# Experts' loop of a ViT tower with a mixture of experts: the one-hot table behind the second silu, and the down products in another order

## The chip, the cores and the metric

One core of a Trainium2 chip (trn2) runs the whole program in one launch. The metric is the device time of the execution in microseconds (us), the median of several runs.

## What is computed

The program is an image tower: a tokenizer with windowed attention, a second attention with a top-k mask, and then a mixture-of-experts layer over 2,080 tokens (32 images of 65) of 192 features. The change touches the last part alone. Cut to that part, the reference is:

```python
xb = x[token_buf].reshape(E, CAP, H)              # rows of each expert: E = 128, CAP = 192, H = 192
gu = jnp.einsum('ech,ehf->ecf', xb, W_gate_up)    # f = 2 * 464
g, u = jnp.split(gu, 2, axis=-1)
inter = jax.nn.silu(g) * u
yb = jnp.einsum('eci,eih->ech', inter, W_down)    # i = 464
yb = yb * w_buf.reshape(E, CAP, 1)
routed = jnp.zeros((T, H), x.dtype).at[token_buf].add(yb.reshape(E * CAP, H))
shared = jax.nn.silu(x @ Wsg) * (x @ Wsu) @ Wsd
return (routed + shared).reshape(B, S, H)
```

Only experts to which a token was routed are worked on. With these inputs there are 20 of them, in 10 passes of a loop of two.

## The kernel before

The first three quarters of the program (tokenizer, attentions, router, shared expert) go tile by tile, in an order of stages that is written out by hand. The experts' loop follows. Each engine has its own copy of the loop (`Fori`, 10 passes, `s` = 0 and 1 inside), its instructions stand in program order, and the engines wait for each other by semaphores alone. `v` numbers the experts from 1, and most buffers come in two, by `s`.

For expert `v` the engines do this:

- **TensorE (PE).** Gate and up products in two halves `r` = 0 and 1. Each half has 4 products over the first 128 features (L999) and 4 over the other 64 (L1004), into the banks `big[r]`; the semaphore `eup{r}` tells that a half is done. Between the halves, and behind the L1004 of the first, stands `slots_of` (L928): 34 small bf16 products of a one-hot table that is two experts ahead give the rows' numbers and weights. Behind the second half come four transposes of the next expert's gathered rows (`gathered`, L937, semaphore `xe_T`), and then the down products, again by halves of the inner features. A half waits for `einner{r}`, and has two products with 128 columns of rows (L1014), and two with the other 64 rows (L1017). These last two go to partitions 0 to 63 and 64 to 127 of one bank and are called a pair here. A matmul of float32 shows as two records in the trace.
- **ScalarE (ACT).** The tanh of each half (L1195), the copy of the transposed rows to SBUF (L1125, `xeT_ready`, for the next expert), and, once `down_mm` is there, the scaled result `y` (L1199, L1200, semaphore `y_early`).
- **VectorE (DVE).** For each half the silu (L1636) and the product with `u` (L1640), which sends `einner{r}`. Behind the first half: two small copies for the add (L1644, L1645), `indices_of` (L1559 to L1565), which makes the row numbers for GpSimd's gather, and the generator `slots_of`, which makes the one-hot table of expert `v + 3`. `slots_of` reads the expert's number (L1540, `value_load`), copies its slots (L1542, `twice`), compares them with a row of numbers for tiles 0 to 7 (L1548, 128x1536) and yields. The rest of it, tiles 8 to 16 (L1548, 128x1728) and a copy of weights (L1552, `hot_ready`), runs behind the second half. Last comes the upper part of `y` (L1652), which waits for `y_early` and sends `y_done`.
- **GpSimd (POOL).** The gathers of expert `v + 2` (L1769), behind `index_ready`, and the adds of `y` to the output by indirect DMA (L1807), behind `y_done`.
- **SyncE (SP).** The loads of an expert's weights, one expert ahead: gate and up behind `eup1`, down behind `down_mm`.

The PSUM banks are `lists_bank` (p_small, one per `s`) for the row lists and transposes, and `aux` (p_small for one `s`, p_shared for the other) for the down products. They are four banks.

Of the kernel before, what the change touches and what calls it, by code (L numbers as in the profile page):

```python
# [6 lines left out]
D = 192  # L7
# [6 lines left out]
E, TOPE, CAP = 128, 6, 192  # L14
# [15 lines left out]
NSC, NIC = IS // SC, I // SC  # L30
# [302 lines left out]
def tower_kernel(nc, a, out):  # L333
# [4 lines left out]
    with ctx:  # L338
# [18 lines left out]
        def carve(start, rows, *dims, dt=f32):  # L357

            n = 1
            for d in dims:  # L360
                n *= d
            n = n if dt == f32 else n // 2
            views = [x[0:rows, start:start + n] for x in arena]
            if dt != f32:
                views = [x.bitcast(dt) for x in views]
            if len(dims) == 2:
                views = [x.rearrange("p (a b) -> p a b", b=dims[1]) for x in views]
            return views, start + n
# [146 lines left out]
        w_dn, at = carve(at, SC, NIC, D)  # L515
        xg, at = carve(at, 128, 2, DX)
        einner, at = carve(at, SC, NIC, CAP)
# [8 lines left out]
        lists_bank, aux = [small[1], small[2]], [small[0], sh_bank]  # L526
# [15 lines left out]
        def S(name):  # L542
            return named[name]
# [128 lines left out]
        def _(pe):  # L672
            mm, tr = nc.tensor.matmul, nc.tensor.transpose
# [250 lines left out]
            def slots_of(s, v):  # L924
                pe.wait_ge(S("hot_ready"), v)
                for h in range(2):
                    for t in range(NT):
                        last = mm(lists_bank[s][:, 400 + 6 * h:406 + 6 * h], hot[s][:, t, 128 * h:128 * h + 128], rhs[s][:, t, :],  # L928
                                  start=(t == 0), stop=(t == NT - 1))
                last.then_inc(S("index_mm"), 1)  # L930

            def gathered(s, gather_value, v):
                pe.wait_ge(S(f"gathered{s}"), gather_value)
                for h in range(2):
                    for k in range(2):
                        rows = PARTS[h].stop - PARTS[h].start
                        last = tr(lists_bank[s][:, k * CAP + 128 * h:k * CAP + 128 * h + rows],  # L937
                                  xg[s][0:rows, h, k * 128:(k + 1) * 128], ident[0:rows, 0:rows])
                last.then_inc(S("xe_T"), 1)
# [49 lines left out]
            with pe.Fori(0, n2) as i:  # L989
                for s in range(2):  # L990
                    v = 2 * i + s + 1
                    pe.wait_ge(S(f"w_loaded{s}"), 80 * i + 80)
                    pe.wait_ge(S("xeT_ready"), v)
                    for r in range(2):
                        pe.wait_ge(S(f"einner{r}"), v)
                        for j in range(2):
                            for bank in range(2):
                                c = bank * I + (2 * r + j) * SC
                                mm(big[r][0:SC, bank, j * CAP:(j + 1) * CAP], w_gu[s][:, c:c + SC], xeT[s][:, 0, :],  # L999
                                   start=(j == 0), stop=False)  # L1000
                        for j in range(2):
                            c = (2 * r + j) * SC
                            for bank, rows in enumerate((slice(0, DB), slice(DB, 2 * DB))):
                                last = mm(big[r][0:SC, bank, j * CAP:(j + 1) * CAP], w_gu_late[s][rows, c:c + SC],  # L1004
                                          xeT[s][rows, 1, :], start=False, stop=(j == 1))
                        last.then_inc(S(f"eup{r}"), 1)
                        if r == 0:
                            slots_of(s, v + 2)
                    gathered(1 - s, 32 * i + 32 + 32 * s, v + 1)
                    pe.wait_ge(S("y_done"), v)  # L1010
                    for r in range(2):
                        pe.wait_ge(S(f"einner{r}"), v + 1)
                        for c in range(2 * r, 2 * r + 2):
                            mm(aux[s][:, 0:D], einner[s][:, c, 0:128], w_dn[s][:, c, :], start=(c == 0), stop=False)  # L1014
                        for c in range(2 * r, 2 * r + 2):
                            half = slice(64 * (c % 2), 64 * (c % 2) + 64)
                            last = mm(aux[s][half, D:2 * D], einner[s][:, c, 128:CAP], w_dn[s][:, c, :],  # L1017
                                      start=False, stop=(c >= NIC - 2))
                    last.then_inc(S("down_mm"), 1)

# [182 lines left out]
        def _(dve):  # L1204
# [330 lines left out]
                tt(h3_cls[:], small[1][0:B, 0:D], cls_row[:], ALU.add).then_inc(S("c_h3_ready"), 1)  # L1535
                yield from router_in(1, 1, B)

            def slots_of(j, s, v):

                e = dve.value_load(lists[0:1, bass.ds(j, 1)] if not isinstance(j, int) else lists[0:1, j:j + 1],  # L1540
                                   min_val=0, max_val=E)
                V.tensor_copy(slot_twice[s][:], slot[:, :, bass.ds(e, 1)].to_broadcast([128, NT, 2])).then_inc(S("twice"), 1)  # L1542
                dve.wait_ge(S("twice"), v)
                pairs = "p t (c two) -> p t c two"
                for tiles in (slice(0, HOT_FIRST), slice(HOT_FIRST, NT)):
                    n = tiles.stop - tiles.start
                    shape = [128, n, CAP // 2, 2]
                    tt(hot[s][:, tiles, 0:CAP].rearrange(pairs, two=2),  # L1548
                       iota_b[:].rearrange("p (c two) -> p c two", two=2).unsqueeze(1).to_broadcast(shape),
                       slot_twice[s][:, tiles, :].unsqueeze(2).to_broadcast(shape), ALU.is_equal)  # L1550
                    if tiles.stop == NT:
                        V.tensor_copy(rhs[s][:, :, 3:6], wsplit[:, :, bass.ds(e, 1), :].squeeze(2)).then_inc(S("hot_ready"), 1)  # L1552
                    yield

            def indices_of(s, v):

                dve.wait_ge(S("index_mm"), v)
                p = lists_bank[s][:, 400:412].rearrange("p (h c) -> p h c", c=6)
                stt(slot_a[s][:].unsqueeze(2), p[:, :, 2:3], 1.0, dummy_f[:].unsqueeze(2), ALU.subtract, ALU.mult)  # L1559
                V.reduce_sum(slot_w[s][:].unsqueeze(2), p[:, :, 3:6], axis=AX.X)  # L1560
                V.tensor_copy(slot_b[s][:].unsqueeze(2), p[:, :, 1:2]).then_inc(S("index_part"), 1)
                dve.wait_ge(S("index_part"), 2 * v - 1)
                tt(slot_a[s][:], slot_a[s][:], slot_b[s][:], ALU.add).then_inc(S("index_part"), 1)
                dve.wait_ge(S("index_part"), 2 * v)
                stt(index[s][:].unsqueeze(2), p[:, :, 0:1], 64.0, slot_a[s][:].unsqueeze(2), ALU.mult, ALU.add)\  # L1565
                    .then_inc(S("index_ready"), 1)
# [62 lines left out]
            with dve.Fori(0, n2) as i:  # L1629
                for s in range(2):  # L1630
                    v = 2 * i + s + 1
                    slots = slots_of(2 * i + s + 3, 1 - s, v + 3)
                    for r in range(2):
                        g, u = (big[r][0:SC, b, 0:2 * CAP] for b in range(2))
                        dve.wait_ge(S(f"eth{r}"), v)
                        stt(eth[r][:], eth[r][:], 1.0, g, ALU.add, ALU.mult).then_inc(S("esilu"), 1)  # L1636
                        dve.wait_ge(S("esilu"), 2 * v - 1 + r)
                        if r == 0:
                            dve.wait_ge(S("down_mm"), v)
                        tt(einner[s][:, 2 * r:2 * r + 2, :].rearrange("p c n -> p (c n)"), eth[r][:], u, ALU.mult)\  # L1640
                            .then_inc(S(f"einner{r}"), 1)
                        if r == 0:
                            dve.wait_ge(S("add_done"), v)
                            V.tensor_copy(add_index[s][:], index[s][:])  # L1644
                            ts(add_w[s][:], slot_w[s][:], 0.5, None, op0=ALU.mult).then_inc(S("kept"), 1)  # L1645
                            dve.wait_ge(S("kept"), v)
                            indices_of(s, v + 2)
                        if r == 0:
                            next(slots)
                    run(slots)  # L1650
                    dve.wait_ge(S("y_early"), v)
                    stt(y[s][0:64, 1, :], aux[s][64:128, D:2 * D], add_w[s][0:64, 1:2], y[s][0:64, 1, :], ALU.mult, ALU.add)\  # L1652
                        .then_inc(S("y_done"), 1)
# [235 lines left out]
```

## Time and profile before

| | |
|---|---|
| median of 3 runs | 936.86 us (936.58 to 936.96) |
| the profiled execution | 934.52 us |
| its span, first to last instruction | 932.7 us |
| experts' loop, from the first L999 to the end of the last L1017 | about 186 us of it, 20 experts |
| PE, DVE, ACT, POOL busy over the span | 89%, 77%, 37%, 33% |

The profiled execution stands 2.34 us under the median, of which the span leaves out 1.8 us ahead of the first and behind the last instruction. Busy time is an average over stages with different limits. The loop is read by itself in what follows: rows of one expert in order of time, which tell at each step what started when, and what it had waited for.

### The profile page before, as it was taken

How to read it: one execution, taken by the hardware profiler on the slowest of the kernel's cores; microseconds unless marked ns; L12 is line 12 of the kernel's file. 1: busy time of each engine (PE TensorE's matmuls, PEld its weight loads, DVE VectorE, ACT ScalarE, POOL GpSimd, SP SyncE). 2: the span in 40 equal slices, each digit the busy share in tenths (PEclk: the TensorE clock that was granted, in tenths of full speed). 3: DMA queues.
4: the chain of work that ended last, by engine and by line, in shares of the span. 5: the costliest groups of instructions: out<-in, count | busy, mean ns of one | idle time of the engine just before them, and what ended most of it. 6: DMA issues, size and time to landing. Idle time of an engine off the chain costs nothing.

```text
span 932.7 us, 22271 instructions
## 1 busy us (share of the span) xinstructions
PE 830.9 (89%) x7603; PEld 731.8 (78%) x7603; DVE 722.6 (77%) x3781; ACT 345.7 (37%) x971; POOL 307.7 (33%) x354
## 2 busy tenths in 40 slices
PE   1687899899899899899899999999999999999993
PEld 1576688788788788888789989998879767676762
DVE  3356899999899899999999979799675465656562
ACT  0335554544544544545445344432210122222220
POOL 7021213403313223224123131121121276766664
PEclk8699999999999999999999999999998899999997
DMA  7410000101101101001001100010112466666651
GB/s 222 117 52 1 2 27 23 40 17 37 30 17 36 30 11 39 17 24 34 26 23 44 31 6 21 22 45 20 45 28 64 112 160 144 160 144 160 144 129 24
DMA packets 48231, 54.25 MB, mean 58 GB/s; under 512 B 9013, under 2 KB 41531, under 8 KB 48108
## 3 DMA queue, kind: packets, MB, share of 16 engines
q1 hardware_dynamic: 39180, 43.89, 16.4%
q0 software_dynamic: 6352, 7.62, 5.6%
q10 hardware_dynamic: 2608, 1.60, 0.7%
q8 instruction: 48, 0.79, 0.4%
q14 instruction: 43, 0.35, 0.1%
HBM read 42.40 MB, written 10.69 MB: 57 GB/s over the span
## 4 chain that ended last, share of the span: by engine, by line
DVE 48%; PE 38%; issue 5%; ACT 4%; SPq 2%; DVEq 1%; POOL 0%; DMA 0%; ACTq 0%; POOLq 0%
DVE b_arena L1500 9%; PE p_big L999 3%; PE p_shared L831 3%; DVE b_top_a L1486 3%; PE p_big L686 3%; PE p_shared L832 3%; PE p_big L687 2%; DVE b_top_d L1486 2%; PE p_shared L837 2%; DVE b_arena L1548 2%; DVE b_top_b L1486 2%; DVE b_top_c L1486 2%; PE p_small L693 2%; DVE b_rstd L1238 2%; PE p_big L1004 2%
## 5 line engine op out<-in xcount | busy, mean ns | idle before, releaser
L1769 POOL DMA_INDIRECT b_arena<-x_rows,b_index x44 | 68.0, 1544 | 49.4 <-DVE b_index L1565 36.6
L686 PE MATMUL p_big<-b_xT,b_ff1a 128*128 128x128 f32 x384 | 77.5, 285 | 1.4 <-ACT b_xT L1029 1.4
L1703 POOL TENSOR_TENSOR b_arena<-b_kY,b_mask_k 64x256 f32<-64x256 f32 x16 | 9.7, 608 | 205.9 <-ACT b_kY L1054 205.9
L687 PE MATMUL p_big<-b_xT,b_ff1b 128*128 128x128 f32 x384 | 76.5, 282 | 0.0
L1029 ACT COPY b_xT<-p_small 128x256 f32<-128x256 f32 (+1 forms) x97 | 35.4, 377 | 83.4 <-PE p_small L677 83.3
L1734 POOL TENSOR_TENSOR b_arena<-b_arena 128x768 f32<-128x768 f32 x16 | 27.0, 1687 | 117.8 <-DVE b_arena L1512 117.8
L686 PEld LDWEIGHTS p_big<-b_xT,b_ff1a 128*128 128x128 f32 x384 | 61.6, 200 | 2.5 <-ACT b_xT L1029 2.5
L999 PE MATMUL p_big<-b_xeT,b_arena 128*116 128x192 f32 x320 | 61.9, 336 | 0.0
L687 PEld LDWEIGHTS p_big<-b_xT,b_ff1b 128*128 128x128 f32 x384 | 60.7, 199 | 0.0
L720 PE MATMUL p_big<-b_arena,b_q_blk 128*128 128x256 f32 (+3 forms) x256 | 48.9, 334 | 12.5 <-ACT b_q_blk L1061 12.4
L720 PEld LDWEIGHTS p_big<-b_arena,b_q_blk 128*128 128x128 f32 x256 | 41.3, 190 | 19.4 <-POOL b_arena L1703 12.6
L999 PEld LDWEIGHTS p_big<-b_xeT,b_arena 128*116 128x116 f32 x320 | 50.1, 180 | 5.6 <-issue 5.6
L867 PE MATMUL p_small<-b_patch_w,b_xp 128*128 128x192 f32 x192 | 36.8, 344 | 12.1 <-DMA b_pe<-in_pe 10.3
L1548 DVE TENSOR_TENSOR b_arena<-b_iota_b,b_slot_twice 128x1536 bf16<-128x1536 bf16 (+1 forms) x46 | 46.1, 1005 | 0.8
L1111 ACT ACTIVATE b_th<-p_shared 116x256 f32<-116x256 f32 (+1 forms) x50 | 18.9, 378 | 69.6 <-PE p_shared L832 62.1
L867 PEld LDWEIGHTS p_small<-b_patch_w,b_xp 128*128 128x128 f32 x192 | 32.5, 198 | 13.4 <-issue 10.2
L1500 DVE MATCH_REPLACE8 b_arena<-b_top_c,b_arena 128x65 f32<-128x65 f32 x208 | 41.7, 210 | 0.0
L1500 DVE MATCH_REPLACE8 b_arena<-b_top_b,b_arena 128x65 f32<-128x65 f32 x208 | 41.2, 211 | 0.0
L1500 DVE MATCH_REPLACE8 b_arena<-b_top_a,b_arena 128x65 f32<-128x65 f32 x208 | 41.2, 212 | 0.0
L837 PE MATMUL p_shared<-b_wsd,b_inner 116*128 116x192 f32 (+1 forms) x208 | 39.9, 349 | 0.8 <-DVE b_inner L1316 0.8
L1078 ACT ACTIVATE b_arena<-b_arena 128x768 f32<-128x768 f32 (+1 forms) x32 | 28.1, 877 | 31.6 <-DVE b_arena L1448 17.8
L1807 POOL DMA_INDIRECT out_rows<-b_hid,b_add_index x20 | 30.6, 1532 | 25.2 <-issue 25.2
(379 smaller groups left out, 2548.1 us busy)
## 6 DMA issues: line engine op xcount, KB each, us to landing
b_arena<-in_w_gate_up SPq DMA_DIRECT2D x20, 464.0 KB
b_arena<-in_w_down SPq DMA_DIRECT2D x20, 336.0 KB
b_xp<-in_xp SPq DMA_DIRECT2D x16, 384.0 KB, 3.1
b_arena<-in_w_gate_up SPq DMA_DIRECT2D x40, 116.0 KB
xT_rows<-b_xmT SPq DMA_DIRECT2D x16, 128.0 KB, 1.8
b_xT_late<-xT_rows SPq DMA_DIRECT2D x16, 128.0 KB, 2.2
h_rows<-b_h SPq DMA_DIRECT2D x16, 96.0 KB, 1.6
x_rows<-b_xm SPq DMA_DIRECT2D x32, 48.0 KB, 2.0
```

Of the source, the lines that this page charges most:

```text
L686: mm(o, ff1a[:, c * 128:(c + 1) * 128], xTa[s][:], start=True, stop=False)
L687: last = mm(o, ff1b[:, c * 128:(c + 1) * 128], xTb[s][:], start=False, stop=True)
L720: last = mm(big[s][:, g, at:(4 + 2 * m) * keys], q_blk[s][:, m, g, :], k[:, g, :, :].rearrange("p j k -> p (j k)"), start=True, stop=True)
L837: last = mm(shared_bank(v, 4)[0:rows, 0:D], inner[:, c, 0:rows], wsd[:, c, :], start=(c == 0), stop=(c == NSC - 1))
L867: last = mm(small[2][:, 0:D], xp[:, c, :], patch_w[:, c, :], start=(c == 0), stop=(c == KC - 1))
L999: mm(big[r][0:SC, bank, j * CAP:(j + 1) * CAP], w_gu[s][:, c:c + SC], xeT[s][:, 0, :], start=(j == 0), stop=False)
L1029: cp((xT[s] if to is None else to)[:, 0:256].rearrange(both, t=128)[:, :, 0:rows], small[s][:, 0:256].rearrange(both, t=128)[:, :, 0:rows] ...
L1486: last = V.max(top[:, 8 * h:8 * h + 8], src[:, h * NKEY:(h + 1) * NKEY])
L1500: last = V.match_replace(work[:, h * NKEY:(h + 1) * NKEY], top[:, 8 * h:8 * h + 8], src[:, h * NKEY:(h + 1) * NKEY], -3e38)
L1548: tt(hot[s][:, tiles, 0:CAP].rearrange(pairs, two=2), iota_b[:].rearrange("p (c two) -> p c two", two=2).unsqueeze(1).to_broadcast(shape), ...
L1769: G.indirect_dma_start(xg[s][0:rows, h, :], None, x_rows[:, :], bass.IndirectOffsetOnAxis(index[s][0:rows, h:h + 1], 0)).then_inc(S(f"gath ...
L1807: G.indirect_dma_start(out[:, :], bass.IndirectOffsetOnAxis(add_index[s][0:rows, h:h + 1], 0), y[s][0:rows, h, :], None, compute_op=ALU.ad ...
```

## The change

Two edits, both in the loop. On VectorE, `slots_of` gets a second place to yield, behind the copy `twice`, which the loop alone uses. So `next(slots)` ahead of the second silu issues the number's load and the copy, and both compares stand behind the second half's product. On TensorE, the down products of the first half come ahead of the next rows' transposes, and both pairs of both halves stand together at the end.

```diff
-                    gathered(1 - s, 32 * i + 32 + 32 * s, v + 1)
                     pe.wait_ge(S("y_done"), v)
                     for r in range(2):
                         pe.wait_ge(S(f"einner{r}"), v + 1)
                         for c in range(2 * r, 2 * r + 2):
                             mm(aux[s][:, 0:D], einner[s][:, c, 0:128], w_dn[s][:, c, :], start=(c == 0), stop=False)
-                        for c in range(2 * r, 2 * r + 2):
-                            half = slice(64 * (c % 2), 64 * (c % 2) + 64)
-                            last = mm(aux[s][half, D:2 * D], einner[s][:, c, 128:CAP], w_dn[s][:, c, :],
-                                      start=False, stop=(c >= NIC - 2))
+                        if r == 0:
+                            gathered(1 - s, 32 * i + 32 + 32 * s, v + 1)
+                    for c in range(NIC):
+                        half = slice(64 * (c % 2), 64 * (c % 2) + 64)
+                        last = mm(aux[s][half, D:2 * D], einner[s][:, c, 128:CAP], w_dn[s][:, c, :],
+                                  start=False, stop=(c >= NIC - 2))
                     last.then_inc(S("down_mm"), 1)
...
-            def slots_of(j, s, v):
+            def slots_of(j, s, v, early=False):
...
                 V.tensor_copy(slot_twice[s][:], slot[:, :, bass.ds(e, 1)].to_broadcast([128, NT, 2])).then_inc(S("twice"), 1)
+                if early:
+                    yield
                 dve.wait_ge(S("twice"), v)
...
-                    slots = slots_of(2 * i + s + 3, 1 - s, v + 3)
+                    slots = slots_of(2 * i + s + 3, 1 - s, v + 3, True)
```

TensorE's instructions around the down products of the first expert of a pass (s = 0), as a difference; L937 are the transposes, L1014 and L1017 the down products of before, L1013 and L1018 the same products in the changed file, and x2 or x4 counts products, not records:

```order
 L999 MATMUL p_big<-b_xeT,b_arena 116x192 x4
 L1004 MATMUL p_big<-b_xeT,b_arena 116x192 x4
+L1011 REGISTER_ALU
+L1013 MATMUL p_small<-b_arena 128x192 x2
 L933 ISA
 L937 MATMUL p_small<-b_ident,b_arena 128x128 x2
 L937 MATMUL p_small<-b_ident,b_arena 128x64 x2
-L1012 REGISTER_ALU
-L1014 MATMUL p_small<-b_arena 128x192 x2
-L1017 MATMUL p_small<-b_arena 64x192 x2
-L1014 MATMUL p_small<-b_arena 128x192 x2
-L1017 MATMUL p_small<-b_arena 64x192 x2
+L1013 MATMUL p_small<-b_arena 128x192 x2
+L1018 MATMUL p_small<-b_arena 64x192 x4
```

The first two down products have moved ahead of the transposes, and the two pairs have become one run of four products at the end. No product is added or taken away.

VectorE's instructions between the slots' copy and the upper part of `y`, in the kernel before:

```order
L1542 COPY b_slot_twice<-b_slot 128x34
L1543 REGISTER_ALU
L1548 TENSOR_TENSOR b_arena<-b_iota_b,b_slot_twice 128x8x192
L1636 SCALAR_TENSOR_TENSOR b_inner<-b_inner,p_big 116x384
L1640 TENSOR_TENSOR b_arena<-b_inner,p_big 116x384
L1548 TENSOR_TENSOR b_arena<-b_iota_b,b_slot_twice 128x9x192
L1552 ISA
L1552 COPY b_rhs<-b_wsplit 128x17x3
L1652 SCALAR_TENSOR_TENSOR b_hid<-p_small,b_add_w,b_hid 64x192
```

The same stretch of VectorE in the changed kernel, whose lines stand one to three further down in the file:

```order
L1543 COPY b_slot_twice<-b_slot 128x34
L1639 SCALAR_TENSOR_TENSOR b_inner<-b_inner,p_big 116x384
L1643 TENSOR_TENSOR b_arena<-b_inner,p_big 116x384
L1546 REGISTER_ALU
L1551 TENSOR_TENSOR b_arena<-b_iota_b,b_slot_twice 128x8x192
L1551 TENSOR_TENSOR b_arena<-b_iota_b,b_slot_twice 128x9x192
L1555 ISA
L1555 COPY b_rhs<-b_wsplit 128x17x3
L1655 SCALAR_TENSOR_TENSOR b_hid<-p_small,b_add_w,b_hid 64x192
```

The compare of 8 tiles has moved from ahead of the second silu to behind the product that follows it; the rest keeps its order.

## Rows read from the trace of the kernel before

**Rows 1.** Loop: us; PE, PEld, DVE, ACT, POOL busy; PEclk; DMA share; GB/s

```profile
731.70:917.60 185.90, 177.26 (x1721) 132.13 (x1720) 110.55 (x320) 42.96 (x98) 121.84 (x78) 1.00 0.61 140
```

**Rows 2.** Waits, 745 to 915 us: who waited for whom, us in total, times, longest

```profile
PEld p_small L1014 <- DVE b_arena L1640: 7.4, 9, 0.8
PEld p_shared L1014 <- DVE b_arena L1640: 6.6, 9, 0.7
```

**Rows 3.** The chain that ended last, in one expert: start us, us, what

```profile
793.22 0.20 DVE b_slot_twice L1542
...
793.44 0.96 DVE b_arena L1548
794.40 0.47 DVE b_inner L1636
...
794.90 0.56 DVE b_arena L1640
```

**Rows 4.** TensorE's timeline, the same expert (start, us, records; idle before, releaser)

```profile
787.50 1.56 PE L999 MATMUL p_big<-b_xeT,b_arena 128*116 128x192 f32 x8
...
792.17 0.91 PE L1004 MATMUL p_big<-b_xeT,b_arena 64*116 64x192 f32 x8
793.01 0.70 PE L937 MATMUL p_small<-b_ident,b_arena 128*128 128x128 f32 x4
793.64 0.92 PE L1014 MATMUL p_small<-b_arena 116*128 116x192 f32 x4
...
794.49 0.20 PEld L1017 LDWEIGHTS p_small<-b_arena 116*64 116x64 f32 x4 [0.23 <-issue]
794.49 0.55 PE L1017 MATMUL p_small<-b_arena 116*64 116x192 f32 x4
795.50 0.92 PE L1014 MATMUL p_small<-b_arena 116*128 116x192 f32 x4 [0.47 <-DVE b_arena L1640]
796.35 0.55 PE L1017 MATMUL p_small<-b_arena 116*64 116x192 f32 x4
...
796.83 1.56 PE L999 MATMUL p_big<-b_xeT,b_arena 128*116 128x192 f32 x8
```

**Rows 5.** ScalarE's and VectorE's timeline, the same expert

```profile
789.94 0.49 ACT L1195 ACTIVATE b_hid<-p_big 116x384 f32<-116x384 f32 x1 [1.54 <-PE p_big L1004]
790.47 0.55 DVE L1636 SCALAR_TENSOR_TENSOR b_hid<-b_hid,p_big 116x384 f32<-116x384 f32 x1 [1.61 <-ACT b_hid L1195]
...
791.05 0.55 DVE L1640 TENSOR_TENSOR b_arena<-b_hid,p_big 116x384 f32<-116x384 f32 x1
...
793.12 0.49 ACT L1195 ACTIVATE b_inner<-p_big 116x384 f32<-116x384 f32 x1 [2.69 <-PE p_big L1004]
...
793.75 0.48 ACT L1125 COPY b_xeT<-p_small 128x384 f32<-128x384 f32 x1
...
795.37 1.05 DVE L1548 TENSOR_TENSOR b_arena<-b_iota_b,b_slot_twice 128x1728 bf16<-128x1728 bf16 x1
...
796.34 0.19 DVE L1552 COPY b_rhs<-b_wsplit 128x51 bf16 x1
...
797.76 0.42 DVE L1652 SCALAR_TENSOR_TENSOR b_hid<-p_small,b_add_w,b_hid 64x192 f32<-64x192 f32 x1 [1.24 <-ACT b_hid L1200]
```

**Rows 6.** TensorE's timeline, the expert before it (the other s)

```profile
778.25 1.56 PE L999 MATMUL p_big<-b_xeT,b_arena 128*116 128x192 f32 x8
...
786.18 0.92 PE L1014 MATMUL p_shared<-b_arena 116*128 116x192 f32 x4 [0.39 <-DVE b_arena L1640]
```

**Rows 7.** TensorE's timeline: the first half of the first expert and of the last

```profile
731.73 1.56 PE L999 MATMUL p_big<-b_xeT,b_arena 128*116 128x192 f32 x8
...
908.29 1.56 PE L999 MATMUL p_big<-b_xeT,b_arena 128*116 128x192 f32 x8
```

**Rows 8.** Transposes ahead of the loop, and the granted clock there (columns as rows 1)

```profile
726.56 1.07 PE L937 MATMUL p_small<-b_ident,b_arena 128*128 128x128 f32 x4
...
726.00:728.00 2.00, 2.00 (x10) 1.40 (x11) 0.44 (x2) 0.56 (x2) 0.00 (x0) 0.50 0.93 267
```

## The prediction

> **What bounds the kernel now.** I read three views: the busy table of the loop, the waits, and then, in order of time, the chain and the timelines of one expert. The table shows TensorE busy for 177.26 of the loop's 185.90 us, with the granted clock at 1.00, its upper level of 2.4 GHz [rows 1]. So TensorE is nearly the bound but not quite: 8.64 us, 0.43 us an expert, are left. The waits tell where they lie. The weight loads of the down products wait for VectorE's product L1640, 18 times in the window, 14.0 us together [rows 2]; the matmuls themselves show 0.47 and 0.39 us as idle before them [rows 4, 6]. The chain names the cause. In the expert that starts at 787.50 it runs on VectorE through the slots' copy (793.22), the first compare (793.44), the second silu (794.40) and the product (794.90) [rows 3], and reaches TensorE at 795.50 [rows 4]. The tanh that this silu needs had started at 793.12 and took 0.49 us [rows 5], so it was done at 793.61. The silu stood 0.8 us behind a table that nobody needs until the next expert's turn. This is what the reader is to see: a wait of TensorE for VectorE, and in it an instruction that has nothing to do with the product waited for.
>
> **The clock of one expert.** I count from its first L999, at 787.50 [rows 4]. The transposes start at 793.01, that is +5.51, right behind the gate and up products. L1014 of the second half starts at 795.50, +8.00, and the next L999 at 796.83, +9.33. The other `s` has 7.93 for the same step (778.25 to 786.18) and a period of 9.25 (778.25 to 787.50) [rows 4, 6]. Over the loop, first L999 to last, there are 19 periods in 176.56 us, 9.29 each [rows 7].
>
> **Edit 1, the table behind the second silu.** The first compare (0.96 us, [rows 3]) leaves the path to `einner1`. What is late next is the tanh. In the first half the silu starts 0.53 us after the tanh (789.94 to 790.47, [rows 5]). The same step puts the second silu at 793.12 + 0.53 = 793.65, where VectorE is free since 793.42 [rows 3]. From silu to product it is 0.58 us in the first half (790.47 to 791.05, [rows 5]); the second half has the silu in the chain from 794.40 and the product at 794.90, 0.50 [rows 3], but the chain counts the silu only from the end of the compare. I take 0.58, and keep 0.50 as the lower bound. From product to L1014 it is 0.60 (794.90 to 795.50). That gives 793.65 + 0.58 + 0.60 = 794.83, or +7.33, a gain of 0.67 us for this `s`. The chain hangs on TensorE's own +5.51 now, so the other `s` gets +7.33 too, against 7.93: a gain of 0.60. The mean is 0.64.
>
> Would TensorE be ready for it? In the old order its first pair starts at 794.49 and, as the second pair shows (796.35, next work at 796.83), hands over 0.48 us later, at 794.97, +7.47 [rows 4]. So edit 1 by itself would make TensorE the bound: +7.47 against 8.00 and 7.93, a gain of 0.50 us an expert, 10 us in all.
>
> **Edit 2, the down products' order.** Ahead of the second L1014 now stand the first L1014 (0.85 us to the next group, 793.64 to 794.49) and the transposes (0.63 us, 793.01 to 793.64) [rows 4]. TensorE is ready by 793.01 + 0.85 + 0.63 = 794.49 at the latest, 0.34 us ahead of 794.83. So it still waits, and what ends the wait is VectorE, at +7.33. Behind it come L1014 (0.85) and four pair products instead of two. The price of a run of that length is read from L1004, which also works in parts of the array side by side: 8 records hand over 0.84 us after their start (792.17 to 793.01), 4 records of L1017 after 0.48 [rows 4]. So the two products that were moved here cost 0.36 us, all on the path, where before they lay ahead of the wait, on it only in part. The new period is 7.33 + 0.85 + 0.84 = 9.02 us for both `s`, against 9.29. **Edit 2 thus gives back about half of edit 1**: 0.22 us an expert against edit 1 by itself (7.47 + 0.85 + 0.48 = 8.80), and by itself it would cost 0.36.
>
> The bounds of the 0.36: below, 0.24, half of the 0.48 that a pair takes now; above, 0.62, as if the four records did not run side by side at all and took L1014's 0.85 less the 0.23 for which the weight load sits idle at the changeover [rows 4]. The row of L1004 is nearest: the same number of records, also side by side, with rows of the array split instead of columns.
>
> The timeline also shows the price of changing over between whole and split array: the weight load of L1017 sits idle for 0.23 us ahead of it [rows 4]. 
> **What is hidden.** The transposes end later, near +7.0 instead of +6.1. Their copy takes 0.48 us [rows 5], so the next rows are there at about +7.6 and wanted at +9.02. VectorE's table ends later: product at 794.23, first compare 0.47 later as now (794.90 to 795.37), then 0.96, 0.97 (L1548's second start at 795.37 to L1552 at 796.34 is the pattern, [rows 5]) and 0.19, so about 796.82, +9.32. The table is wanted when the next expert's first half is through, where its tanh starts, +2.44 after that expert's L999 (787.50 to 789.94) [rows 4, 5]. `y` asks for VectorE only behind ScalarE's part, 0.93 us after the next L999 (796.83 to 797.76) [rows 4, 5]: +9.95. So 0.6 us of cover is left; were it gone, `y_done` and GpSimd's adds would slip by the rest. The weights' DMAs are issued at the same events as before, and the DMA share is 0.61 [rows 1].
>
> **The sum.** 20 experts (the last one's down products end the loop, so it counts): 20 x 0.27 = 5.4 us, with the gain per step 20 x (0.64 - 0.36) = 5.6. I take 5.5. The profiled execution goes from 934.52 to 929.0 us. It lies 2.34 us under the median of 936.86, so the median goes to **931.4 us**.
>
> **The rivals.** What a measurement here can tell from no change is about 0.2%, 1.9 us.
> - *The pairs do not fold.* Two pairs that add to the same half of a bank, one right behind the other, might not run as L1004 does. At the upper bound of 0.62 the gain is 20 x 0.02 = 0.4 us, at 0.50 it is 20 x 0.14 = 2.8 us, 934.1. For it: before, each pair had other work between it and the next. Against: a pair's products already go two records to each half of the bank, and the four hand over after 0.48 where L1014's four take 0.85 [rows 4]. Chance 0.09 for a gain between 1.9 and 4.4 us, 0.03 for less.
> - *VectorE's own chain takes over.* The slots' copy ends 0.2 us ahead of the silu (793.42 and 793.65). If the compares behind the product push `y`, and with it the release of L1644, by over those 0.6 plus 0.2 us, the silu waits again. It would be worth 0.27 us an expert to cancel all: 936.9, no change. It needs 0.8 us that no row gives. Chance 0.03.
> - *The clock falls (slower).* The new order puts the transposes next to the wait. Ahead of the loop, at a granted clock of 0.50 (1.2 GHz), four transpose records took 1.07 us against 0.70 at 1.00 [rows 4, 8]. TensorE's busy time of an expert is 177.26 / 20 = 8.9 us; by that ratio, 1.53, an expert at the lower level costs 4.7 us more, and at twice the time 8.9. So it decides from the second such expert on. With five of the 20 it is 5 x 4.7 - 5.5 = 18 us, 954.9. Against it: the clock stands at 1.00 over the whole loop, with a wait of 0.39 to 0.47 us in an expert [rows 1, 4, 6], and the new wait is 0.34 and the changeovers fewer. Chance 0.04. "TensorE: Matmul & The Clock Gate" of the Trainium skill, part 4, says that transposes do not count as work for the clock, which speaks against this change; no row here singles them out.
> - *More than forecast.* If the silu and product keep the 0.50 step and the moved products take 0.24, the period is 7.25 + 0.85 + 0.72 = 8.82: 20 x 0.47 = 9.4 us, 927.5. Chance 0.04 for over 6.6 us.
>
> **How the numbers follow.** The forecast has a chance of 0.77, for a gain of 4.4 to 6.6 us, 930.3 to 932.5. Folding less takes the range up to 934.0, the short step down to 929.6; what is left out is the no-change cases, the clock and the far end of the gain. Faster by over 0.2%: 0.77 + 0.09 + 0.04 = 0.90. Within: 0.03 + 0.03 = 0.06. Slower: 0.04.
>
> **What would show it.** In the trace of the changed kernel: the second silu starts 0.53 us behind its tanh and no compare ahead of it; L1013's second start at +7.33 in both `s`, with an idle time of some 0.3 to 0.5 us before it, still ended by the product (now L1643); L1018 x8 hands over after 0.84; periods of 9.02, alike for both `s`; ACT's copy of the next rows ends over 1 us before they are wanted; L1655 still released by ScalarE, not by the table. I am wrong if L1018 takes over 1.0 us, if the wait before the second L1013 has another releaser, if L1655 starts right behind L1555, or if the granted clock is under 1.00.

## The result and the profile after

| | before | changed |
|---|---|---|
| median, first group of runs | 936.91 us | 929.86 us |
| ratio, 95% interval | | 0.9922, 0.9906 to 0.9939 |
| median, second group of runs (`full_again`) | 936.34 us | 930.87 us |
| ratio, 95% interval | | 0.9936, 0.9922 to 0.9949 |
| profiled execution, its span | 934.52, 932.7 us | 930.37, 928.5 us |

The changed kernel is faster by 7.1 us in one group and 5.5 in the other, and neither interval holds a ratio of 1. The loop's own share is read without that scatter from the trace. TensorE's timeline of the changed kernel, first half of the first and of the last expert:

```profile
733.62 1.68 PE L999 MATMUL p_big<-b_xeT,b_arena 128*116 128x192 f32 x8
...
904.59 1.56 PE L999 MATMUL p_big<-b_xeT,b_arena 128*116 128x192 f32 x8
```

19 periods (from one expert's first L999 to the next's) take 170.97 us, 8.998 each, where they took 176.56 us, 9.293 each [rows 7]. The first of them takes 9.12 us, all others 8.99. The difference times 20 is 5.9 us. The loop begins at 733.62 here and at 731.73 there, though nothing ahead of it was changed, and so the two profiled executions are only 4.15 us apart. Over the profiled kernels of this study the loop begins anywhere from 730.55 to 736.35 us. Below, the price of an edit is therefore read from the period, and the timed runs are set beside it.

The timeline of one expert, all engines, from its first L999 to the upper part of its `y` (in the changed file L1013 and L1018 are the down products, L1196 the tanh, L1639 the silu, L1643 the product, L1551 the compares, L1772 the gathers, L1655 the upper part of `y`):

```profile
787.70 1.56 PE L999 MATMUL p_big<-b_xeT,b_arena 128*116 128x192 f32 x8
...
793.21 0.92 PE L1013 MATMUL p_small<-b_arena 116*128 116x192 f32 x4
793.32 0.49 ACT L1196 ACTIVATE b_inner<-p_big 116x384 f32<-116x384 f32 x1 [2.69 <-PE p_big L1004]
793.42 0.19 DVE L1543 COPY b_slot_twice<-b_slot 128x34 bf16 x1 [0.65 <-issue]
...
793.79 1.02 POOL L1772 DMA_INDIRECT b_arena<-x_rows,b_index  x1 [0.30 <-issue]
...
793.85 0.55 DVE L1639 SCALAR_TENSOR_TENSOR b_inner<-b_inner,p_big 116x384 f32<-116x384 f32 x1 [0.24 <-ACT b_inner L1196]
793.96 0.65 PE L937 MATMUL p_small<-b_ident,b_arena 128*128 128x128 f32 x4
...
794.43 0.55 DVE L1643 TENSOR_TENSOR b_arena<-b_inner,p_big 116x384 f32<-116x384 f32 x1
...
794.90 1.92 DVE L1551 TENSOR_TENSOR b_arena<-b_iota_b,b_slot_twice 128x1536 bf16<-128x1536 bf16 x2
...
795.04 0.92 PE L1013 MATMUL p_small<-b_arena 116*128 116x192 f32 x4 [0.43 <-DVE b_arena L1643]
...
795.89 0.87 PE L1018 MATMUL p_small<-b_arena 116*64 116x192 f32 x8
796.69 1.56 PE L999 MATMUL p_big<-b_xeT,b_arena 128*116 128x192 f32 x8
796.74 0.19 DVE L1555 COPY b_rhs<-b_wsplit 128x51 bf16 x1
...
797.62 0.42 DVE L1655 SCALAR_TENSOR_TENSOR b_hid<-p_small,b_add_w,b_hid 64x192 f32<-64x192 f32 x1 [0.69 <-ACT b_hid L1201]
```

Read it against [rows 3 to 5], counting from the first L999. The second silu now waits for its tanh (0.24 us idle, released by ScalarE) and starts at +6.15. In the kernel before it started at +6.82, as VectorE's timeline shows (the chain of [rows 3] has it at 794.40, since it counts it only from the end of the compare, which this silu overlaps by 0.08 us):

```profile
794.32 0.55 DVE L1636 SCALAR_TENSOR_TENSOR b_inner<-b_inner,p_big 116x384 f32<-116x384 f32 x1
```

The second L1013 starts at +7.34 instead of +8.00. Behind it come 0.85 and 0.80 us, and the next expert starts at +8.99. The chain that ended last shows what has left the path:

```profile
784.33 0.50 ACT b_inner L1196
784.83 0.02 issue
784.85 0.56 DVE b_inner L1639
785.42 0.02 issue
785.44 0.57 DVE b_arena L1643
786.01 0.04 issue
786.05 0.92 PE p_shared L1013 x4
```

The slots' copy and the compare, which stood ahead of the silu in [rows 3], are gone, and the tanh of the second half is in their place. What is left is TensorE's wait for tanh, silu and product in a row. The busy table of the loop (columns as in [rows 1]) still has 8.7 us in which TensorE is idle, as many as before:

```profile
733.60:913.60 180.00, 171.31 (x1721) 135.14 (x1720) 110.38 (x319) 42.88 (x98) 108.49 (x78) 1.00 0.61 144
```

So the change did not fill TensorE's wait, it moved it. In the expert of [rows 4] TensorE was idle from +7.53 to +8.00; now it is from +6.91 to +7.34, since a pair of products that stood ahead of the wait stands behind it. The busy time fell from 177.26 us [rows 1] to 171.31 for the same products, and the idle time stayed. A changeover is a step from products that use the whole array to products on a part of it, or back; the new order has two less an expert, and that the busy time fell by these is likely and not shown by itself. The experiments ask what each edit did, and whether the rest of the wait can be had.

### The profile page after: what moved, and what is told of

It reads as the page before. It is cut to its first block, busy times and chain, and to the rows that moved or that the text cites. A ratio compares the mean times of both kernels' runs of the same rounds, so it can differ in the third digit from the quotient of the medians.

```text
span 928.5 us, 22271 instructions
## 1 busy us (share of the span) xinstructions
PE 828.2 (89%) x7603; PEld 736.9 (79%) x7603; DVE 722.5 (78%) x3781; ACT 345.2 (37%) x971; POOL 294.3 (32%) x354
## 4 chain that ended last, share of the span: by engine, by line
PE 47%; DVE 42%; issue 4%; ACT 4%; SPq 2%; POOL 0%; DMA 0%; DVEq 0%; ACTq 0%; POOLq 0%
DVE b_arena L1501 9%; PE p_big L999 6%; PE p_big L1004 4%; PE p_big L686 3%; PE p_big L687 3%; PE p_shared L831 3%; DVE b_top_a L1487 3%; PE p_shared L832 3%; PE p_shared L837 2%; DVE b_top_d L1487 2%; PE p_small L928 2%; DVE b_top_c L1487 2%; PE p_small L693 2%; DVE b_rstd L1239 2%; DVE b_top_b L1487 2%
## 5 line engine op out<-in xcount | busy, mean ns | idle before, releaser
L1772 POOL DMA_INDIRECT b_arena<-x_rows,b_index x44 | 54.9, 1247 | 50.4 <-DVE b_index L1568 37.6
L999 PE MATMUL p_big<-b_xeT,b_arena 128*116 128x192 f32 x320 | 62.0, 337 | 0.0
L720 PEld LDWEIGHTS p_big<-b_arena,b_q_blk 128*128 128x128 f32 x256 | 41.3, 190 | 19.3 <-POOL b_arena L1706 12.5
L999 PEld LDWEIGHTS p_big<-b_xeT,b_arena 128*116 128x116 f32 x320 | 50.2, 180 | 5.9 <-issue 5.9
L1551 DVE TENSOR_TENSOR b_arena<-b_iota_b,b_slot_twice 128x1536 bf16<-128x1536 bf16 (+1 forms) x46 | 44.3, 1002 | 0.1
L837 PE MATMUL p_shared<-b_wsd,b_inner 116*128 116x192 f32 (+1 forms) x208 | 42.0, 361 | 0.8 <-DVE b_inner L1317 0.8
```

Source lines behind the costliest of these rows:

```text
L720: last = mm(big[s][:, g, at:(4 + 2 * m) * keys], q_blk[s][:, m, g, :], k[:, g, :, :].rearrange("p j k -> p (j k)"), start=True, stop=True)
L837: last = mm(shared_bank(v, 4)[0:rows, 0:D], inner[:, c, 0:rows], wsd[:, c, :], start=(c == 0), stop=(c == NSC - 1))
L1551: tt(hot[s][:, tiles, 0:CAP].rearrange(pairs, two=2), iota_b[:].rearrange("p (c two) -> p c two", two=2).unsqueeze(1).to_broadcast(shape), ...
L1772: G.indirect_dma_start(xg[s][0:rows, h, :], None, x_rows[:, :], bass.IndirectOffsetOnAxis(index[s][0:rows, h:h + 1], 0)).then_inc(S(f"gath ...
```

## The experiments

All edits are to the changed kernel, unless it says otherwise. Periods, in us, are from the first to the last first-half L999, in one profiled execution of each kernel. "Gain" is 20 times the difference to the 9.293 of the kernel before. Each median stands beside that of the kernel before from the same group of runs, and both are of 5 to 15 runs where an interval is given.

| kernel | period | gain by it | median, that of the kernel before | ratio, 95% interval |
|---|---|---|---|---|
| changed kernel | 8.998 | 5.9 | 929.86, 936.91 | 0.9922 (0.9906 to 0.9939) |
| the same again (`full_again`) | 8.992 | 6.0 | 930.87, 936.34 | 0.9936 (0.9922 to 0.9949) |
| table_alone | 8.787 | 10.1 | 929.03, 938.16 | 0.9893 (0.9867 to 0.9918) |
| order_alone | 9.616 | -6.5 | 945.53, 938.16 | 1.0073 (1.005 to 1.0096) |
| pairs_by_half | 8.667 | 12.5 | 923.90, 938.16 | 0.9846 (0.9818 to 0.9874) |
| one_half_at_a_time | 9.006 | 5.7 | 934.00, 938.16 | 0.9954 (0.9935 to 0.9973) |
| slots_late | 8.530 | 15.3 | 921.68, 936.34 | 0.9846 (0.9833 to 0.986) |
| second_load | 9.185 | 2.2 | 934.34 (one run), 936.34 | none |
| three_on_one_half | 9.311 | -0.4 | 936.36 (one run), 936.34 | none |
| late_y | 8.992 | 6.0 | 927.96, 935.45 (one run each) | none |
| two_more_compares | 8.994 | 6.0 | 931.16, 936.50 (one run each) | none |

`full_again` tells how far a period can be trusted: the same kernel in another group of runs gives 8.992 for 8.998, and the difference lies in the first period alone. A period of 8.99 us and a ratio of 0.992 to 0.994 had been expected of it.

**The table's move by itself.** TensorE's part of the change is undone.

```diff
+                    gathered(1 - s, 32 * i + 32 + 32 * s, v + 1)
                     pe.wait_ge(S("y_done"), v)
                     for r in range(2):
...
-                        if r == 0:
-                            gathered(1 - s, 32 * i + 32 + 32 * s, v + 1)
-                    for c in range(NIC):
+                        for c in range(2 * r, 2 * r + 2):
...
```

> Only the first compare moves behind the second silu; TensorE keeps its old order (transposes, then products and pair by halves). My theory (the second silu waited for a table that nobody needs; the new order of products gives part of that back): TensorE becomes the bound, the second half's products start at +7.47 instead of +7.34 but are followed by one pair only (0.48 us instead of 0.80), so the period is 8.80 us against 8.99 with both edits, 9.29 before: about 4 us faster than the full change, some 925.9 us beside 929.9 and 936.9. Rival (the new order is what pays, the table alone gives little): the time stays within 2 us of before, 935 us or more.

TensorE's timeline of this kernel, the expert's first products and then from the first pair on:

```profile
780.28 1.56 PE L999 MATMUL p_big<-b_xeT,b_arena 128*116 128x192 f32 x8
...
787.27 0.55 PE L1017 MATMUL p_shared<-b_arena 116*64 116x192 f32 x4
787.75 0.92 PE L1014 MATMUL p_shared<-b_arena 116*128 116x192 f32 x4
788.60 0.55 PE L1017 MATMUL p_shared<-b_arena 116*64 116x192 f32 x4
789.07 1.56 PE L999 MATMUL p_big<-b_xeT,b_arena 128*116 128x192 f32 x8
```

L1014 carries no idle time: it starts 0.48 us after the first pair, at +7.47. TensorE is the bound. The period is 8.787, the gain by it 10.1 us. By the periods, one edit alone gives more than both. The timed runs lean the same way, but their intervals overlap the changed kernel's by a little: 0.9867 to 0.9918 here, 0.9906 to 0.9939 there, and 0.9922 to 0.9949 in `full_again`.

**The new order by itself.** The kernel before, with TensorE's part of the change.

> Only TensorE's order changes; VectorE keeps the first compare ahead of the second silu. My theory: the second half's products start where they did (+8.00 and +7.93, set by VectorE), and behind them come 0.85 + 0.80 us instead of 0.85 + 0.48, so the period grows by 0.32 us: 20 x 0.32 = 6.4 us slower than before, some 943 us. Rival (fewer changeovers of the array, two less an expert, pay wherever they fall): 3 to 6 us faster than before, 931 to 934 us.

```profile
782.13 0.92 PE L1013 MATMUL p_small<-b_arena 116*128 116x192 f32 x4 [1.09 <-DVE b_arena L1641]
782.97 0.87 PE L1018 MATMUL p_small<-b_arena 116*64 116x192 f32 x8
783.77 0.42 PE L999 MATMUL p_big<-b_xeT,b_arena 128*116 128x192 f32 x1
```

(The view ends there, so that it shows one record of the next L999.) The wait ahead of the second products has grown to 1.09 us, from 0.47 [rows 4]: what stood ahead of it now stands behind it. The period is 9.616, 0.32 us longer than before, as expected, and the timed ratio, 1.005 to 1.0096, shows the loss too. Fewer changeovers did not pay here. The rival falls.

**Pairs by half.** The new order, but with each pair behind its own half; the first pair then stands behind the transposes.

```diff
                         if r == 0:
                             gathered(1 - s, 32 * i + 32 + 32 * s, v + 1)
-                    for c in range(NIC):
-                        half = slice(64 * (c % 2), 64 * (c % 2) + 64)
+                        for c in range(2 * r, 2 * r + 2):
+                            half = slice(64 * (c % 2), 64 * (c % 2) + 64)
...
```

> The full change, but each half's pair of products stands behind that half again: first products, transposes, first pair, second products, second pair. My theory: the first pair now fills the 0.43 us in which TensorE still waits; the second products could start at 5.51 + 0.76 + 0.63 + 0.48 = +7.38, just behind VectorE's +7.34, and behind them come 0.85 + 0.48: period 8.71 us, 20 x 0.28 = 5.6 us faster than the full change, some 924 us. Rival (every changeover costs what it drains, and four pairs in one run are cheapest): not faster than the full change, 930 us or more.

```profile
779.36 1.56 PE L999 MATMUL p_big<-b_xeT,b_arena 128*116 128x192 f32 x8
...
786.20 0.55 PE L1018 MATMUL p_shared<-b_arena 116*64 116x192 f32 x4
786.71 0.92 PE L1013 MATMUL p_shared<-b_arena 116*128 116x192 f32 x4
787.55 0.55 PE L1018 MATMUL p_shared<-b_arena 116*64 116x192 f32 x4
788.03 1.56 PE L999 MATMUL p_big<-b_xeT,b_arena 128*116 128x192 f32 x8
```

No idle time stands ahead of L1013, which starts at +7.35, and only one pair follows. The period is 8.667. The first pair takes 0.51 us where it stands, and L1013 starts no later by it (+7.34 in the changed kernel): TensorE and VectorE now come to this point together. The 0.33 us between the two periods is what the run of four gives away.

**Two that test the run of four.** The pair products in the order 0, 2, 1, 3, and three of four on one half of the partitions.

```diff
-                    for c in range(NIC):
+                    for c in (0, 2, 1, 3):
                         half = slice(64 * (c % 2), 64 * (c % 2) + 64)
```

> The full change with the four pair products in the order 0, 2, 1, 3, so that the two that go to the same half of the partitions are neighbours. My theory (the run of four takes 0.80 us because products to different halves run side by side): neighbours on one half run one behind the other, the run takes up to twice its streaming time, 0.80 + 0.2 to 0.5 us, so 4 to 10 us slower than the full change, 934 to 940 us. Rival (the 0.80 is a price per product that does not depend on the halves): no difference, 930 us.

```diff
                     for c in range(NIC):
-                        half = slice(64 * (c % 2), 64 * (c % 2) + 64)
+                        half = slice(64 * (c // 3), 64 * (c // 3) + 64)
```

> The full change, but three of the four pair products go to the lower half of the partitions and one to the upper; so one part of the inner features is added to the wrong rows of the output, its work is unchanged. If products to different halves run side by side and those to one half one behind the other, three in a row take 1.5 times as long as two: the run of four goes from 0.80 to 1.1 us or so, the period to 9.3. If the price of such a product does not depend on the half, the period stays 8.99.

TensorE's timeline, first `one_half_at_a_time` (both views end within the next L999):

```profile
792.87 0.88 PE L1018 MATMUL p_small<-b_arena 116*64 116x192 f32 x8
793.68 1.40 PE L999 MATMUL p_big<-b_xeT,b_arena 128*116 128x192 f32 x7
```

and `three_on_one_half`:

```profile
788.04 1.19 PE L1018 MATMUL p_shared<-b_arena 116*64 116x192 f32 x8
789.16 1.07 PE L999 MATMUL p_big<-b_xeT,b_arena 128*116 128x192 f32 x5
```

The order alone changes the run from 0.80 to 0.81 us, and the period by 0.01. Three on one half make it 1.12 us and the period 9.311. So the halves do run side by side, as a price of 0.80 for eight records says, but the products need not be neighbours for that; what counts is how many go to each half. By the trace a half takes up its records 0.16 us apart, and two records more on one half make the 0.32 us. In the order 0, 2, 1, 3 the first two records of the run start 0.01 us apart, as they do in the changed kernel; with three on one half the second starts only 0.21 us behind the first. So a product for the free half does not wait for the one ahead of it in program order.

By this my expectation for the order was wrong, and its rival was right about the time for the wrong reason: the price does depend on the halves. The timed median, 934.0 us, is in what had been expected (934 to 940) all the same: it shows 4.2 us of gain where the period says 5.7. The profiled execution is the fastest of the ten, 927.56 us, and whether the others had its period isn't known. In one point the expectation of `three_on_one_half` is wrong as well. No part of the inner features goes to wrong rows, since L1201 and L1655 add the two halves of the bank for the same rows of `y`; only the share of each half changes.

**TensorE's wait filled with work that has to be done.** The 34 small products move from between the halves to behind the first down products, and VectorE makes the indices behind its second product.

```diff
                         last.then_inc(S(f"eup{r}"), 1)
-                        if r == 0:
-                            slots_of(s, v + 2)
...
                         if r == 0:
+                            slots_of(s, v + 2)
                             gathered(1 - s, 32 * i + 32 + 32 * s, v + 1)
...
                             ts(add_w[s][:], slot_w[s][:], 0.5, None, op0=ALU.mult).then_inc(S("kept"), 1)
-                            dve.wait_ge(S("kept"), v)
-                            indices_of(s, v + 2)
-                        if r == 0:
                             next(slots)
+                        else:
+                            dve.wait_ge(S("kept"), v)
+                            indices_of(s, v + 2)
```

> The full change, and the 34 small products of the row lists moved from between the two gate and up halves to behind the first down products (ahead of the transposes); VectorE makes the indices behind the second product. My theory (TensorE's wait for the second product is 0.43 us of the 8.99; anything that has to be done anyway can fill it): the work of TensorE is 8.99 - 0.43 = 8.56 us an expert, and the period is that: 20 x 0.43 = 8.6 us faster than the full change, some 921 us. Rival (the gathers, now issued some 3 us later, land behind the time at which the transposes want them, and TensorE waits for them): period over 8.99, 930 us or more.

```profile
776.75 1.56 PE L999 MATMUL p_big<-b_xeT,b_arena 128*116 128x192 f32 x8
...
781.40 0.92 PE L1011 MATMUL p_shared<-b_arena 116*128 116x192 f32 x4
...
782.16 1.00 PE L928 MATMUL p_small<-b_rhs,b_arena 128*128 128x6 bf16 x34
...
783.01 0.69 PE L937 MATMUL p_small<-b_ident,b_arena 128*128 128x128 f32 x4
...
783.63 0.92 PE L1011 MATMUL p_shared<-b_arena 116*128 116x192 f32 x4
...
784.48 0.87 PE L1017 MATMUL p_shared<-b_arena 116*64 116x192 f32 x8
784.78 1.02 POOL L1771 DMA_INDIRECT b_arena<-x_rows,b_index  x1 [2.24 <-DVE b_index L1567]
```

No row of TensorE has idle time, and in its busy table TensorE is busy for 170.70 of 170.70 us. The period is 8.530 (8.56 was expected). The first gather starts at +8.03, 1.9 us later than in the changed kernel (+6.09), and the rows are still there in time. With a ratio of 0.9846 (0.9833 to 0.986) this version beats both kernels: the same instructions, 14.7 us under the kernel before and 9.2 under `full_again`, timed beside it.

**The margin ahead of the second silu.** One more load of the expert's number.

```diff
                 if early:
+                    dve.value_load(lists[0:1, bass.ds(j, 1)], min_val=0, max_val=E)
                     yield
```

> The full change, with one more load of the expert's number (some 0.6 us on VectorE's queue, its result unused) ahead of the second silu. My theory (the slots' copy ends 0.23 to 0.3 us ahead of the silu, that much is margin): the silu slips by 0.6 - 0.27, the period grows by 0.3 to 0.4 us, the loop by 6 to 8 us. Rival (VectorE's chain has plenty of room there now): no difference, period 8.99.

```profile
785.46 0.49 ACT L1196 ACTIVATE b_inner<-p_big 116x384 f32<-116x384 f32 x1 [2.69 <-PE p_big L1004]
...
786.14 0.55 DVE L1640 SCALAR_TENSOR_TENSOR b_inner<-b_inner,p_big 116x384 f32<-116x384 f32 x1 [0.47 <-ACT b_inner L1196]
```

The period is 9.14 and 9.23 in turn for the two `s`, 9.185 in the mean, where 8.99 stood. The silu starts 0.68 us behind its tanh instead of 0.53. The load ends in those 0.47 us of idle time, where the changed kernel has 0.24 and 0.32 us for the two `s`: that was the margin. The load itself takes the 0.6 us that I took for it (785.50 to 786.09 in the trace), but it starts beside the slots' copy, and only 0.47 us of it stand behind the copy. So the loss is 0.19 us and not 0.3 to 0.4.

**The cover behind the table.** First with loads, then with real work for VectorE.

```diff
                     run(slots)
+                    for _ in range(4):
+                        dve.value_load(lists[0:1, bass.ds(2 * i + s, 1)], min_val=0, max_val=E)
                     dve.wait_ge(S("y_early"), v)
```

> The full change, with four more loads of the expert's number on VectorE's queue behind the table and ahead of the upper part of y (unused results, some 0.4 us each by what one cost in second_load). My theory (0.69 us of idle time cover the later table, and behind that GpSimd's adds have room too): y's upper part starts about 1 us later than in the full change, the adds start as much later, and the period stays 8.99 us. Rival of the prediction (a late y holds up the release of the add's copies and with them the second silu): the period grows, towards 9.3 or more.

```profile
786.20 0.42 DVE L1657 SCALAR_TENSOR_TENSOR b_inner<-p_shared,b_add_w,b_inner 64x192 f32<-64x192 f32 x1 [0.69 <-ACT b_inner L1201]
```

Inconclusive: `y` was not late. It still starts 0.94 us after the next L999 (785.26) with the same idle time. In the trace the four loads run from 783.38 to 785.83 in VectorE's queue, 0.6 us apart: beside the compares up to 785.40, and then within the idle time ahead of `y`. So the delay was made of compares.

```diff
                     run(slots)
+                    for n in range(2):
+                        ...
+                        tt(spare[n][:]..., iota_b[:]..., slot_twice[1 - s][:, HOT_FIRST:NT, :]..., ALU.is_equal)
                     dve.wait_ge(S("y_early"), v)
```

> The full change with two more compares of 9 tiles into spare tiles (unused) behind the table, ahead of the upper part of y: real VectorE work of about 1.9 us, since the loads of late_y ran beside the compares and delayed nothing. My theory (0.69 us of idle cover, and more behind it in GpSimd): the upper part of y starts some 1.2 us later, now right behind VectorE's own work, GpSimd's adds as much later, and the period stays 8.99 us. Rival of the prediction (a late y holds up the release of the add's copies and with them the second silu): the period grows by 0.3 us or more.

```profile
776.45 1.92 DVE L1552 TENSOR_TENSOR b_arena<-b_iota_b,b_slot_twice 128x1536 bf16<-128x1536 bf16 x2
776.57 1.73 POOL L1778 DMA_INDIRECT b_arena<-x_rows,b_index  x1 [0.30 <-issue]
...
780.41 0.42 DVE L1661 SCALAR_TENSOR_TENSOR b_hid<-p_small,b_add_w,b_hid 64x192 f32<-64x192 f32 x1
...
781.91 1.61 POOL L1816 DMA_INDIRECT out_rows<-b_hid,b_add_index  x1 [1.68 <-issue]
```

Now `y` has no idle time ahead of it and starts 3.82 us behind the second L1014 (776.59) instead of 2.58 behind the second L1013 in the changed kernel, 1.24 us later; the adds follow. The period stays: 8.994. So a `y` that is 1.24 us later costs nothing. How much later it could be, and how late the table itself could be, no run shows.

## Why the prediction was right

- **Edit 1.** The silu starts 0.53 us after its tanh: 793.32 to 793.85. Silu to product is 0.58 us, product to the second products 0.61. The sum said +7.33 for both `s`; measured is +7.34, with one period, 8.99, for both where there had been two. The 0.50 kept as a lower bound for silu to product was the chain's way of counting, as supposed: the silu of before starts at 794.32, 0.58 us ahead of its product, and it stood 0.71 us behind its tanh's end rather than 0.8.
- **Edit 2.** The run of four hands over after 0.80 us; 0.84 was taken from L1004. The moved pair costs 0.32, not 0.36. This is the term that was a little too large; with the +7.34 the mean period came out 0.02 us shorter than said, 0.4 us of the 5.9. The bounds, 0.24 and 0.62, held it.
- **Ready before it is wanted.** TensorE was to be ready 0.34 us or more ahead. It waits 0.43, since the first down products hand over to the transposes after 0.75 us (793.21 to 793.96) and not after the 0.85 that they take when a pair follows.
- **Edit 2 gives back part of edit 1.** Predicted: 10 us for the table alone, a loss of 0.36 an expert for the order alone, 0.22 given back when both are made. Shown by their periods: 10.1 us, 0.32, and 0.21 (8.998 against 8.787). The timed medians of the two single edits go the same way, 9.1 us faster and 7.4 slower, with wider intervals.
- **Hidden parts.** The copies of the next rows, the table and `y` stayed hidden: `y` starts at +9.92 (+9.95 said), still released by ScalarE. `two_more_compares` shows that there is more room than the 0.6 to 0.8 us that were counted; the rival that hung on it is refuted as far as a `y` 1.24 us late.
- **The clock.** It stands at 1.00 over the loop in all these traces, though the transposes now stand by the wait. What the prediction cites on transposes from "TensorE: Matmul & The Clock Gate" of the Trainium skill, part 4, had no effect to show here, with a wait of 0.43 us.
- **The drain rule.** The Trainium skill says in "TensorEngine Tiling (Array Packing)", section Key Properties, that a change of tiling mode drains the engine. The prediction reckoned 6 us from it for changeovers saved anywhere, with 0.15 us each, for which it names no row. TensorE's busy time did fall by 5.9 us, 0.15 for each of the 40, but that is not the cause of the gain: `order_alone` saves as many and is slower, and `pairs_by_half` has one more and is faster. Where TensorE never waits it is otherwise. `table_alone`, `pairs_by_half` and `slots_late` do the same products, are busy throughout, and each has one changeover less than the one named ahead of it; their periods are 8.787, 8.667 and 8.530 us. (The 64-row transposes are counted as work on a part of the array.) So a changeover saved is worth some 0.13 us where TensorE is the bound, an estimate from the first and the last of these periods that puts all of the difference down to changeovers, and nothing where TensorE waits anyway.

The size: 931.4 us was forecast, a gain of 5.5. The loop gained 5.9, the two groups of timed runs 7.1 and 5.5. The step that was off is the 0.84; the rest of the first group's 7.1 us is not in the loop's period. Its cause stays open; the traces differ by several us in what lies ahead of the loop. The first group's 929.86 us lies just under the 930.3 to 932.5 of the forecast itself, and within the range only because that reached down to 929.6 for a rival, shorter steps, which did not happen. That the second group has 5.5 exactly is as much luck. What the runs bear out is the mechanism and the period, 9.02 said and 8.99 measured.

## What to carry to other kernels

When an engine waits for a chain, first take out of the chain what nobody there needs. Then look at what stands ahead of the wait and behind it: independent work belongs ahead, where it fills the wait, and only what needs the late operand behind it. Merging like work into one run saves little and can move it to the wrong side; here this cost 0.2 us of every 9, while moving 1 us of small products into the gap brought 0.47. A period read over twenty experts tells 0.01 us, where whole runs scatter by several us.

## What the runs showed of the hardware

**Products to the two column halves of TensorE overlap without being neighbours.** Two and two took 0.80 us in turn and 0.81 in the order 0, 2, 1, 3; three and one took 1.12, and one half's records start 0.16 us apart.

**A gather's time on GpSimd depends on VectorE's compares.** A gather in the kernel before, issued 0.16 us after the first compare began (793.44, [rows 3]):

```profile
793.60 1.70 POOL L1769 DMA_INDIRECT b_arena<-x_rows,b_index  x1 [0.30 <-issue]
```

It ended at 795.30, 0.90 us after that compare (794.40). With no compare under way when it starts the same gather took 1.02 us (793.79 in the changed kernel). In `two_more_compares` it began at 776.57, 0.12 us after the start of a compare that by the trace ends at 777.41, took 1.73 us, and ended at 778.30, 0.89 us after the compare. In the traces of all these kernels a gather of 128 rows that starts 0.7 to 0.8 us ahead of a compare's end is over 0.89 us behind that end, and the one of 64 rows 0.80 us behind it (0.93 us alone). The gather seems to lose what is left of the compare when it starts. "SBUF — State Buffer" of the Trainium skill, in its part on the port that VectorE and GpSimd share ("SBUF: two separate sides"), says that a VectorE operation with two inputs from SBUF shuts out a GpSimd one that reads SBUF until it ends. The traces agree in these cases. One case does not fit: in `slots_late` the gather at 784.78 begins 0.02 us behind the start of the second compare, and takes 1.02 us beside it, while that compare takes 1.11 us instead of 1.05. That it is the port was not tested by itself. On the profile's page the gathers' busy time falls from 68.0 to 54.9 us for 44. The loop does not wait for them, as `slots_late` shows, where they start 1.9 us later at no cost.

**Loads of a register on VectorE's queue run beside its operations.** A load takes 0.6 us there. Four of them behind 1.9 us of compares, and with 0.69 us of idle time to follow, delayed nothing; one of them ahead of a silu, with only the copy of 0.19 us to run beside, put 0.47 us between copy and silu.
